# First layer's attention: keys and values split and kept in DRAM, split products, mask by TensorE

## What is computed

```python
xn = _layernorm(x)                                   # (2, 1024, 256)
q = einsum('bsh,he->bse', xn, w_q).reshape(b, sq, GROUPS, HPG, KVC)      # 4 groups x 4 heads x 128
k, v = split(einsum('bsh,he->bse', xn, w_kv), 2)     # 4 groups x 128 each
scores = einsum('bqgpd,bkgd->bgqpk', q, k) * SCALE   # SCALE = 128 ** -0.5
scores = where(causal, scores, -inf)
probs = softmax(scores)
ctx = einsum('bgqpk,bkgd->bqgpd', probs, v).reshape(b, sq, HEADS * KVC)
x = x + einsum('bse,eh->bsh', ctx, w_dense) + ffn(xn)
...                                                  # three more layers
```

## Time and profile before

| | before |
|---|---|
| time, median of 3 runs (lowest, highest) | 3837.56 us (3833.1, 3840.24) |
| the profiled execution's own time | 3841.85 us |
| its span, from the first to the last instruction | 3840.0 us |
| granted PE clock, mean over the span | 0.954 |
| busy: PE, PEld, DVE, ACT, POOL | 3466.9, 2618.4, 2420.7, 1537.1, 1403.2 us |
| DMA, whole span | 183.19 MB, mean 48 GB/s |

### The profile page before, as it was taken

One profiled execution on the slowest core, in us unless ns is written; L12 is line 12 of the kernel. 1 busy time (PEld: TensorE's weight loads), 2 busy tenths in 40 slices (PEclk: granted clock), 3 DMA queues, 4 the chain that ended last, 5 costly groups with the idle time before them and its releaser, 6 DMA issues. The chain is left out here.

```text
span 3840.0 us, 66211 instructions
## 1 busy us (share of the span) xinstructions
PE 3466.9 (90%) x21608; PEld 2618.4 (68%) x21608; DVE 2420.7 (63%) x4872; ACT 1537.1 (40%) x2827; POOL 1403.2 (37%) x1083
## 2 busy tenths in 40 slices
PE   6899999999889799999997759999859999699997
PEld 4677777777666688888884335555438888388883
DVE  3556556555433566566665668989468888488883
ACT  2444444444332444444443215666333333233332
POOL 1323333333222566666663320000013444544444
PEclk8999999999999899999998888999979999899998
DMA  0000000000100100000000222222034443144431
GB/s 34 8 4 4 5 3 5 5 3 5 36 0 0 54 18 14 18 18 18 17 16 3 96 110 78 83 82 80 25 115 107 115 115 97 36 107 115 114 97 48
DMA packets 120727, 183.19 MB, mean 48 GB/s; under 512 B 22545, under 2 KB 69777, under 8 KB 120337
## 3 DMA queue, kind: packets, MB, share of 16 engines
q1 hardware_dynamic: 114512, 173.90, 15.0%
q0 software_dynamic: 6144, 8.39, 1.3%
HBM read 153.80 MB, written 28.18 MB: 47 GB/s over the span
## 5 line engine op out<-in xcount | busy, mean ns | idle before, releaser
L447 POOL TENSOR_TENSOR l0h_probs<-l0h_probs,l0h_inv 128x128 f32<-128x128 f32 (+7 forms) x256 | 292.7, 1146 | 586.1 <-DVE l0h_inv L482 586.1
L1798 DVE TENSOR_REDUCE l2h_half<-l2h_s 128x1 f32<-128x512 f32 x512 | 337.5, 686 | 47.5 <-PE l2h_s L1700 46.7
L378 PE MATMUL l0h_sc<-l0a_KT,l0h_QT 128*128 x768 | 298.2, 501 | 29.2 <-ACT l0h_probs L551 27.5
L1785 ACT ACTIVATE l2h_PT<-l2h_s 128x1024 f32<-128x1024 f32 x256 | 248.3, 1022 | 162.4 <-PE l2h_s L1710 162.3
L405 PE MATMUL l0h_cx<-l0h_PT,l0h_VG 128*128 128x128 f32 x2304 | 300.7, 276 | 0.0
L551 ACT ACTIVATE l0h_probs<-l0h_sc,l0h_negtop 128x128 f32<-128x128 f32 (+7 forms) x256 | 189.6, 741 | 245.3 <-DVE l0h_negtop L477 244.8
L405 PEld LDWEIGHTS l0h_cx<-l0h_PT,l0h_VG 128*128 128x128 f32 x2304 | 278.1, 192 | 1.0
L159 POOL TENSOR_TENSOR XN<-XN,n_rstd 128x512 f32<-128x512 f32 x32 | 39.8, 1266 | 595.1 <-DVE n_rstd L140 595.1
L1700 PE MATMUL l2h_s<-l2h_K,l2h_Q 128*128 128x512 f32 x512 | 218.8, 466 | 22.6 <-DMA l2h_K<-l_split 20.3
L475 DVE TENSOR_REDUCE l0h_top<-l0h_sc 128x1 f32<-128x128 f32 (+7 forms) x256 | 194.1, 758 | 8.8
L378 PEld LDWEIGHTS l0h_sc<-l0a_KT,l0h_QT 128*128 128x128 f32 x768 | 126.0, 192 | 106.0 <-issue 63.5
(11 more groups left out here) (407 smaller groups left out, 9017.2 us busy)
## 6 DMA issues: line engine op xcount, KB each, us to landing
l3p_decb<-l_decays SPq DMA_DIRECT2D x128, 256.0 KB, 4.5
l3p_w<-L_w SPq DMA_DIRECT2D x34, 512.0 KB, 3.7
l2h_Q<-l_split SPq DMA_DIRECT2D x64, 256.0 KB
l2h_K<-l_split SPq DMA_DIRECT2D x64, 256.0 KB
l3p_prow<-l_decays SPq DMA_DIRECT2D x128, 128.0 KB, 3.2
l_split<-l2q_hi SPq DMA_DIRECT2D x16, 512.0 KB, 4.0
l_split<-l2q_lo SPq DMA_DIRECT2D x16, 512.0 KB, 3.8
l3p_wgu<-L_ffn_w_gate_up SPq DMA_DIRECT2D x32, 256.0 KB, 4.8
```

The costliest lines, as they stand in the source:

```text
L378: mm = pe.matmul(sc[u % 2][:, lo:lo + n], QT[:, u * P:(u + 1) * P], KT[:, ds(g, 1), b * S + lo:b * S + lo + n], start=True, stop=True)
L447: pool.tensor_tensor(p, p, inv[:, u % 4:u % 4 + 1].to_broadcast([P, keys(u)]), ALU.mult).then_inc(probs_scaled, 1)
L1785: act.activation(PT[:, b, kb, :], s2[kb % 2][:, :], ACT.Exp, scale=L2_SCALE).then_inc(exped, 1)
L1798: dve.reduce_max(half[:, b, t, z:z + 1], bank(slot_of(i))[:, :], AX_X).then_inc(s1_read, 1)
```

## The change

`l0_attn` gets two DRAM tensors, `kd` for the keys and `vd` for the values, each with a high and a low part, and four SBUF tiles of one group: `KH`, `KL` (128 x 2048), `VH`, `VL` (128 x 16 x 128), all fp32r.

In `l0_kv` the values come first, then the keys. Of every accumulated bank ACT rounds the high part to a staging tile (four of each kind) and DVE subtracts it for the low part; SP stores both, 256 KB each: keys in runs of 512 tokens, values in runs of 128 features. When the values and the first group's keys are down (20 of 32 jobs), SP issues the loads of group 0, eight of 512 KB, and goes on storing. The block ends after the last store.

In `l0_heads` the pipeline runs on from head to head in 18 slots: 16 units in the order of tile pairs (0,1), (6,7), (2,3), (4,5) per sequence, and two query slots, in which PE projects one sequence's queries (12 products of 512 columns), ACT rounds the high part with the scale, and DVE makes the low part. Head 0, a loop over heads 1 to 14 and head 15 are written out one after the other. Scores are three fp32r products per chunk of up to 512 keys, and on the diagonal tile PE adds the mask as a product of a bf16 identity with a bf16 mask. DVE takes the negated maximum in one instruction. Probabilities are not scaled; the inverse sum is applied when DVE adds the dense product to `acc`, which holds the layer's result token-wise. Of every transposed tile ACT takes the high part and DVE the low part (`PTH`, `PTL`), so that a bank `tp` is free after both. Values are weighed for two units at once, 256 columns, three fp32r products per key tile (128 columns for the last key tile, which only the second unit sees). The dense product takes the context as the stationary side and 256 columns of dense weights, which are all loaded at the start. At the end PE transposes `acc` (32 transposes) and DVE adds it to `XT` (8 additions). POOL only clears `acc`, ahead of its first weight split, and splits the query weights.

```diff
+def l0_kv(nc, k, a, kd, vd, kv):
...
+        jobs = [("v", t, 0) for t in range(TT)] + [("k", g, j) for g in range(L0_GROUPS) for j in range(NJ)]
+        FIRST = TT + NJ
...
+                for n in range(len(jobs)):
+                    if n == FIRST:
+                        for i in range(NB):
+                            sp.wait_ge(stored[i], 32 * (FIRST // NB))
+                        for b in range(B):
+                            load_keys(sp, kd, kv, 0, b)
+                            load_values(sp, vd, kv, 0, b)
+                    sp.wait_ge(hi_ready, n + 1)
+                    sp.dma_start(target(n, 0), staged(hi, n)).then_inc(stored[n % NB], 16)
+                    sp.wait_ge(lo_ready, n + 1)
+                    sp.dma_start(target(n, 1), staged(lo, n)).then_inc(stored[n % NB], 16)
...
+def l0_heads(nc, k, a, kd, vd, kv):
...
+    UNITS = [(b, t) for b in range(B) for m in (0, 3, 1, 2) for t in (2 * m, 2 * m + 1)]
+    SLOTS = [("unit", i) for i in range(4)] + [("query", 1)] + [("unit", i) for i in range(4, 12)] + [("query", 0)] + [("unit", i) for i in range(12, 16)]
...
+                def scores(h, s, i):
...
+                        pe.matmul(sc[s % 2][:, lo:lo + n], QH[:, q], kv.KH[:, key], start=True, stop=False)
+                        pe.matmul(sc[s % 2][:, lo:lo + n], QH[:, q], kv.KL[:, key], start=False, stop=False)
+                        mm = pe.matmul(sc[s % 2][:, lo:lo + n], QL[:, q], kv.KH[:, key], start=False, stop=not diagonal)
+                        if diagonal:
+                            mm = pe.matmul(sc[s % 2][:, t * P:(t + 1) * P], ident[:, :], causal[:, :], start=False, stop=True)
...
+                def turn_probs(h, i):
...
+                            pe.wait_ge(pt_lo, NT * h + n - 1)
...
+                def weigh_values(h, i):
...
+                    for kb in range(t + 1):
+                        col = slice(0 if kb < t else P, L0_PAIR)
+                        V = b * NQ + kb
+                        pe.matmul(cx[:, col], kv.VH[:, V, :], PTH[:, pair % 2, kb, col], start=(kb == 0), stop=False)
+                        pe.matmul(cx[:, col], kv.VH[:, V, :], PTL[:, pair % 2, kb, col], start=False, stop=False)
+                        mm = pe.matmul(cx[:, col], kv.VL[:, V, :], PTH[:, pair % 2, kb, col], start=False, stop=(kb == t))
...
             @block.tensor
...
+                def step(h, s):
+                    if exists(h):
+                        kind, i = SLOTS[s]
+                        if kind == "unit":
+                            bank_free(h, s)
+                            scores(h, s, i)
+                        elif exists(h + 1 - i):
+                            bank_free(h, s)
+                            project(h + 1 - i, i, sc[s % 2])
+                    if u := unit_at(h, s, 2):
+                        turn_probs(*u)
+                    if u := unit_at(h, s, 5):
+                        dense(*u)
+                    if (u := unit_at(h, s, 3)) and u[1] % 2:
+                        weigh_values(*u)
...
             @block.vector
...
+                def step(h, s):
+                    if exists(h):
+                        kind, i = SLOTS[s]
+                        if kind == "unit":
+                            row_max(h, s, i)
+                        elif exists(h + 1 - i):
+                            low_queries(2 * h + (3 if i == 0 else 2), i, sc[s % 2])
+                    if u := unit_at(h, s, 2):
+                        invert(*u)
+                        low_probs(*u)
+                    if u := unit_at(h, s, 5):
+                        add_dense(*u)
...
             @block.scalar
...
+                def step(h, s):
+                    if u := unit_at(h, s, 2):
+                        high_probs(*u)
+                    if exists(h):
+                        kind, i = SLOTS[s]
+                        if kind == "unit":
+                            exp(h, s, i)
+                        elif exists(h + 1 - i):
+                            high_queries(2 * h + (3 if i == 0 else 2), i, sc[s % 2])
+                        if s == SPLIT_SLOT and exists(h + 1):
+                            split_weights(h + 1)
+                    if (u := unit_at(h, s, 3)) and u[1] % 2:
+                        keep_ctx(*u)
```

More of the change, by code:

```diff
@@ L320, in l0_heads @@
         sc = [st.ps(f"sc{i}", 2 * BANK) for i in range(2)]
         tp = [st.ps(f"tp{i}") for i in range(2)]
[L322 to L327, removed]
@@ new lines, in l0_heads, with back, exists, unit_at @@
+        dense_done, added, cleared, turned_back, x_added = (st.sem(n) for n in ("dense_done", "added", "cleared", "turned_back", "x_added"))
+        def back(h, s, n):
+            return (h, s - n) if s >= n else (h - 1, s - n + NS)
+        def exists(h):
+            return not isinstance(h, int) or 0 <= h <= LAST
+        def unit_at(h, s, n):
+            hh, ss = back(h, s, n)
+            kind, i = SLOTS[ss]
+            return (hh, i) if kind == "unit" and exists(hh) else None
+        def steps(engine, step):
+            for s in range(NS):
+                step(0, s)
+            with engine.Fori(1, LAST) as h:
+                for s in range(NS):
+                    step(h, s)
+            for s in range(NS):
+                step(LAST, s)
+            for s in range(5):
+                step(LAST + 1, s)
@@ new lines, in dense @@
+                def dense(h, i):
+                    if i == 0:
+                        pe.wait_ge(wd_loaded, 16)
+                    pe.wait_ge(ctx_ready, NPAIR * h + i // 2 + 1)
+                    if i or not isinstance(h, int) or h > 0:
+                        pe.wait_ge(added, NU * h + i)
+                    pe.matmul(outp[:, 0:D], ctxT[:, i // 2 % 2, i % 2 * P:(i % 2 + 1) * P], wd[:, ds(h, 1), :].rearrange("p a n -> p (a n)"),
+                              start=True, stop=True).then_inc(dense_done, 1)
@@ new lines, in _ @@
+                project(0, 0, sc[1])
+                pe.wait_ge(mask_here, 1)
+                steps(pe, step)
+                for n in range(NJ * DC):
+                    j, c = divmod(n, DC)
+                    pe.wait_ge(added, NU * L0_HEADS)
+                    wait(pe, x_added, n - 3)
+                    bank = sc[n // 2 % 2][:, n % 2 * BANK:(n % 2 + 1) * BANK]
+                    for i in range(4):
+                        mm = pe.transpose(bank[:, i * P:(i + 1) * P], acc[:, 4 * j + i, c * P:(c + 1) * P], k.ident[:, :])
+                    mm.then_inc(turned_back, 1)
@@ new lines, in invert, with low_probs @@
+                def invert(h, i):
+                    dve.wait_ge(probs_ready, NU * h + i + 1)
+                    dve.reciprocal(inv[:, i % 8:i % 8 + 1], total[:, i % 8:i % 8 + 1]).then_inc(inverted, 1)
+                def low_probs(h, i):
+                    b, t = UNITS[i]
+                    pair = i // 2
+                    for j in range(TILES[i]):
+                        n, m = FIRST_TILE[i] + j, min(4, t + 1 - 4 * j)
+                        dve.wait_ge(pt_hi, NT * h + n + 1)
+                        part = (slice(None), pair % 2, slice(4 * j, 4 * j + m), slice(i % 2 * P, (i % 2 + 1) * P))
+                        dve.tensor_tensor(PTL[part], tp[n % 2][:, 0:m * P].rearrange("p (m n) -> p m n", m=m), PTH[part].bitcast(F32),
+                                          ALU.subtract).then_inc(pt_lo, 1)
```

408 lines of the change are left out of this document (193 added, 215 removed).

## The result

The changed kernel takes 3867.22 us (median of 4 runs, 3864.7 to 3872.46) against 3835.94 for the kernel before beside it (4 runs, 3833.1 to 3840.24): ratio 1.0082, 95% interval 1.0065 to 1.0100. It is 0.8% slower. The profiled execution has a span of 3865.7 us, 25.7 more than before; the medians differ by 31.3, because the execution profiled before took 5.9 us more than the median beside it and this one 0.3.

The account below looks back on a forecast made before the run. It took TensorE to bound the head loop, with idle time between heads. Terms +22, +0.8, +8 and +6.7 gave +37.5 us: 3879 from the profiled execution, 3875 from the median; range 3800 to 3935 for 8 in 10.

Parts of the forecast that it names:

- Keys and values in DRAM: Key and value stage: stores and loads through one queue delay the next stage's first load by 22 us (15 to 55).
- The two hand-overs: Key and value stage: about 2 us without traffic before the loads, and 2 us for the last store to land.
- The rival with values at 137 GB/s: Key and value stage: slow value stores dominate, +33 us, total 3908; inside the forecast's range, no separate chance.
- Memset: Start of the query weights' split: GpSimd's 3.5 us memset stands ahead of it and costs 0.8 us.
- Narrow fp32r products: Head loop, 128 columns: forecast 0.112 us each; rival, like fp32 at 0.224, total 3921, chance 0.20.
- that of wide ones: Head loop rival: 256-column fp32r products cost 0.22 us each, +154 us, total 4029, chance 0.05.
- Entry cost: Head loop, PE: entering fp32r after fp32 products costs 0.09 us, 24 times, 2.2 us a head.
- PE's 51.8: Head loop: PE's work per head after the change, products 49.6 us plus 2.2 for entering fp32r; 0.4 less than before.
- What replaces the idle time: Head loop: query-slot waits for transpose bank (2.0), dense addition (0.9) and small ones (0.5), twice: 6.8 us a head against 5.9.
- After the loop: After the head loop: 32 transposes and 8 VectorE additions turn the sums back, adding 6.7 us.
- The rival that the bank chain does not bind: Head loop: splits pass on faster, PE runs through; 3774 us with 0.5 idle, 3739 without entry cost; chance 0.25.
- break-even point: Head loop: below 4.5 us of PE idle per head the changed kernel would be faster than before.

Follow-up runs that it names:

- kv_group0_kept: Changed kernel with the first key group's split keys and values kept in SBUF, without stores or loads for them: 3845.4 us, ratio 1.0016 to before.
- kv_loads_last: Changed kernel with the eight loads of the first group issued after all 64 stores have landed, not after 40: 3865.6 us, ratio 1.0076 to before.
- add_first: Changed kernel with VectorE's step reordered to row maximum, dense addition, low probabilities, low queries last: 3801.2 us, ratio 0.9914 to before.
- q_low_first: Changed kernel with VectorE making the low probabilities before the low queries in a query slot: 3823.4 us, ratio 0.9958 to before.
- best: add_first plus the first key group kept in SBUF and GpSimd's memset behind its first weight split: 3776.8 us, ratio 0.9846 to before.

## Why the prediction was right, and where not

**Right in the sign and the place.** Slower, because the DRAM round trip and the turning back outweigh what the loop gains. Step by step:

- *Keys and values in DRAM*, +22: it is +28.0 (99.32 to 127.30). The two hand-overs, 2 and 1.5 us without traffic, are the predicted 2 and 2. Too short was the time of the bytes, 61.6: the first 20 jobs move from 56.9 to 93.8, 36.9 us where 28 + 5.5 were counted, since values ran at 285 GB/s and not 300, the first jobs below that, and four key jobs took more than 5.5; loads and 12 key jobs move from 96.0 to 125.8, 29.7 where 11.6 + 16.4 were counted. The other 1.3 us are the first byte, at 56.9 and not 55.6. The rival with values at 137 GB/s falls. That the queue's bytes set the end is shown by kv_group0_kept and kv_loads_last together.
- *Memset*, +0.8: 4.28 - 3.49 = 0.8 us (before, 99.32 to 102.81).
- *Narrow fp32r products*: the rival that they run like fp32 falls, as does that of wide ones. 512, 384, 256 and 128 columns follow each other after 0.23, 0.18, 0.12 and about 0.10 us, a mask product 0.06. With these a head's products are 14.0 (scores and mask), 13.8 (values, 96 x 0.12 + 8 x 0.28) and 20.6, together 48.4 and not 49.6.
- *Entry cost*, 24 x 0.09 = 2.2: the record that I read in the earlier trace rows does not show it. In add_first a dense product (two passes of 0.215 us) starts at 405.31 and so ends at 405.74; the fp32r product behind it is recorded from 405.55 already and its successor from 405.97, 0.23 after 405.74. The first record of such a block starts early, and entering costs nothing there. That PE's 51.8 was still not far off is luck: in add_first, with the clock at 1.00, a head less its named waits is 53.3 - 1.8 = 51.5, that is 3.1 above the products, in many small gaps between groups that the prediction did not count. How they arise stays open.
- *What replaces the idle time*, 6.8 a head: this is the mis-sized term of the loop. The query slots' bank wait is there, 1.85 us against 2.0, 3.9 a head; the dense wait is 1.05 and not 1.8, and the small waits, 1.0 a head in the prediction, come to less than 0.1: 4.9 in all. Against that PE's time beside its waits is 52.4, not 51.8. The difference is the lower clock behind 11 of the 28 idle stretches, 0.6 a head; the prediction had no term for it, and the expectation of q_low_first has it behind each stretch. So 57.27 and not 58.6, and the loop gains 13 us (16 x 0.83) where the prediction had it lose 8.
- *After the loop*, +6.7: 6.5.

The errors, +6 in the stage and -21 in the loop, offset each other in part, and that is luck; the sum of the steps is +22.6 in the profile against +37.5, while the medians differ by 31.3. The rival that the bank chain does not bind falls as stated, since it does bind. Its break-even point, 4.5 us idle a head, looks near at 4.9, but by the prediction's own sum 4.9 gives 37.5 - 16 x 1.9 = +7; the measured +22.6 lies above that by the stage's 6 and by the lower clock's 0.6 a head, so the true break-even point was lower. q_low_first took the kernel past it by a change of VectorE's order alone, to 0.4% under the kernel before.

## What to carry over

Splitting an operand in two puts a second engine in series on every buffer that is emptied; look first at what stands ahead of it in that engine's queue, and put long work that nobody waits for soon (here the low queries) last. Work moved ahead of a long block on PE loses that block as its cover. A round trip through DRAM in one queue costs its bytes wherever the loads stand; keeping the quarter that is needed first on the chip saved 24 of its 28 us.

## What the hardware showed

- Of 28 idle stretches of PE of 1.85 us (changed kernel, 170 to 980 us) 11 were followed by about 3 us at the lower clock level, 0.50, and 17 were not; what tells them apart stays open. With waits of at most 0.9 us (q_low_first) the granted clock from 170 to 980 us was 1.00.
- The two 128-column casts of VectorE took 3.55 and 3.48 us beside GpSimd's 3.51 us memset and 0.23 and 0.22 in best, where the memset comes later. The Trainium skill, in "SBUF — State Buffer", (Who interferes with whom), says that a cast of VectorE can take a port pair that it shares with GpSimd, and that whichever starts second then waits for the whole of the first; the durations here agree.
- Value stores in 512 B runs moved 283 GB/s, in 2 KB runs 383 (524 KB in 1.37 us). The Trainium skill, in "DMA: Bandwidth & Descriptors" (Specifications), puts full line rate at 512 B and above; here 512 B is not enough.
